# Attention kernel: probabilities turned by DMA in every unit, cache pages copied in three stages, planes and weight parts shared out anew

## What is computed

```python
w = weight[adapter_ids]                                  # 8 of 16 matrices of 512x512
x = x + jnp.einsum('bsi,boi->bso', x, w)                 # layer 0

q = einsum('bsd,ed->bse', x, Wq)                         # 32 heads of 128
k = einsum('bsd,ed->bse', x, Wk); v = ... Wv             # 8 heads of 128
q, k = rope(rmsnorm(q, q_norm_w)), rope(rmsnorm(k, k_norm_w))
kc, vc = k_cache[block_table], v_cache[block_table]      # 16 pages of 32 rows a sequence
scores = q @ concat(kc, k).T * SCALE, cache rows beyond cache_seqlens masked
o = softmax(scores) @ concat(vc, v)                      # 4 query heads share a key head
x = x + einsum('bse,de->bsd', o, Wo)                     # layer 1
```

## Time and profile before

| what | value |
|---|---|
| median of 3 runs | 1097.03 us (1094.78 to 1098.75) |
| profiled execution, its time | 1094.0 us |
| its span, first to last instruction | 1092.0 us |
| granted TensorE clock, mean | 0.97 of full speed |
| busy, us: TensorE, VectorE, GpSimd, ScalarE | 977.4, 920.3, 863.5, 796.4 |
| SyncE's DMA queue, share of 16 engines' span | 65.5% |
| ScalarE's DMA queue | 6.1% |
| moved | 173.69 MB in 505733 packets |

### The profile page before, as it was taken

How to read it: one execution, slowest core, us unless ns; L and a number is a source line. 1 busy time by engine, 2 the same in 40 slices (tenths; PEclk the granted TensorE clock), 3 DMA queues, 4 the chain that set the end, 5 groups by cost and what they waited for, 6 DMA issues and landing times.

```text
span 1092.0 us, 20813 instructions
## 1 busy us (share of the span) xinstructions
PE 977.4 (90%) x5617; PEld 559.3 (51%) x5617; DVE 920.3 (84%) x1942; ACT 796.4 (73%) x2202; POOL 863.5 (79%) x1184
## 2 busy tenths in 40 slices
PE   6787997789868999989998999899998999899997
PEld 4344554455434555545554555455555555455554
DVE  6576876578868999989997999979997999899994
ACT  4364655468677888878887888878887888777873
POOL 3656567558858998889898998889888988989881
PEclk9889999899999999999999999999999999999999
DMA  8688977738897777766778677876776777757862
GB/s 256 174 230 239 246 229 221 207 106 160 179 187 137 142 154 157 138 136 142 158 140 162 128 144 157 148 145 140 154 139 139 153 158 140 130 99 133 152 140 64
DMA packets 505733, 173.69 MB, mean 159 GB/s; under 512 B 429121, under 2 KB 487762, under 8 KB 505618
## 3 DMA queue, kind: packets, MB, share of 16 engines
q1 hardware_dynamic: 482752, 149.76, 65.5%
q10 hardware_dynamic: 21714, 20.25, 6.1%
q0 software_dynamic: 1152, 2.36, 0.8%
HBM read 98.11 MB, written 31.86 MB: 119 GB/s over the span
## 4 chain that ended last, share of the span: by engine, by line
PE 42%; DVE 19%; issue 4%; POOL 2%; ACT 2%; DVEq 0%; POOLq 0%; ACTq 0%
PE S L1729 10%; DVE pr L1359 5%; DVE pr L1331 5%; DVE sm L1344 4%; PE Y L1655 4%; PE Y L1657 4%; PE Y L1656 4%; PE Q L1656 3%; PE Q L1655 3%; PE Q L1657 3%; PE O L1655 2%; PE O L1656 2%; PE O L1657 2%; PE T L1661 2%; POOL wl L644 2%
## 5 line engine op out<-in xcount | busy, mean ns | idle before, releaser
L1359 DVE SCALAR_TENSOR_TENSOR pr<-pr,rc,upper 128x640 f16<-128x640 f32 x220 | 235.2, 1069 | 20.5 <-ACT upper L1025 13.8
L1331 DVE CUSTOM_DVE_ANT_0 pr<-S,mask,rst 128x640 f32<-128x640 f32 x256 | 224.4, 876 | 30.8 <-PE S L1729 19.2
L1025 ACT ACTIVATE upper<-pr,rc 128x640 f16<-128x640 f32 x220 | 170.3, 820 | 75.7 <-DVE rc L1347 75.6
L1045 ACT ACTIVATE pr<-pr,nb 128x640 f32<-128x640 f32 x256 | 209.6, 819 | 17.5 <-DVE nb L1331 14.5
L1729 PE MATMUL S<-kh,qh 128*128 128x320 f16 x512 | 113.0, 303 | 41.9 <-DVE nb L1331 41.9
L754 POOL TENSOR_TENSOR m<-m 128x512 f32<-128x512 f32 x63 | 81.7, 1297 | 78.1 <-DVE m L1403 78.1
L1729 PE MATMUL S<-kl,qh 128*128 128x320 f16 x512 | 112.3, 301 | 0.9 <-POOL kl L644 0.9
L1729 PE MATMUL S<-kh,ql 128*128 128x320 f16 x512 | 112.5, 302 | 0.0
L644 POOL TENSOR_TENSOR wl<-wraw,wh 128x512 f16<-128x512 f32 x71 | 104.2, 1468 | 5.9
L1729 PEld LDWEIGHTS S<-kh,qh 128*128 128x128 f16 x512 | 45.9, 99 | 116.1 <-DVE nb L1331 71.1
L1655 PE MATMUL Q<-wh,xh 128*128 128x512 f16 x256 | 99.9, 390 | 4.1 <-issue 2.8
(11 more groups left out here) (218 smaller groups left out, 2719.4 us busy)
## 6 DMA issues: line engine op xcount, KB each, us to landing
wraw<-in_wall SPq DMA_DIRECT2D x74, 256.0 KB, 3.5
cache_rows<-in_kv ACTq DMA_DIRECT2D x80, 224.0 KB
rawk<-cache_rows SPq DMA_DIRECT2D x55, 256.0 KB
vraw<-cache_rows SPq DMA_DIRECT2D x55, 256.0 KB, 4.6
cache_rows<-in_kv SPq DMA_DIRECT2D x36, 224.0 KB
second<-in_lw SPq DMA_DIRECT2D x4, 1024.0 KB
first<-in_lw SPq DMA_DIRECT2D x3, 1024.0 KB
cache_rows<-in_kv SPq DMA_DIRECT2D x16, 192.0 KB, 3.6
```

The costliest lines, as they stand in the source:

```text
L1025: e.activation(upper16[:, g, :], pr[:, slot(u, g), :], ACT.Copy, scale=rc[:, u % 2, g:g + 1]).then_inc(a_f1, 1)
L1045: e.activation(pr[:, slot(u, g), :], pr[:, slot(u, g), :], ACT.Exp, bias=nb[:, u % 2, g:g + 1], scale=-1.0, accum_out=sm[:, u % 2, g:g + 1 ...
L1331: e.tensor_tensor_reduce(pr[:, slot(u, g), :].rearrange("p (a n) -> p a n", a=2), S[:, :, 0:320], mask[:, u % NB, :].rearrange("p (a n) -> ...
L1359: e.scalar_tensor_tensor(out=lower16(u, g), in0=pr[:, slot(u, g), :], scalar=rc[:, u % 2, g:g + 1], in1=upper16[:, g, :], op0=ALU.mult, op ...
```

## The change

- Every unit's probabilities go through `upper_plane`, `lower_plane` and four DMA transposes, into a new tile `turned`. `norm`, `turn_p` and the per-unit `p_hi` and `p_lo` go; the last unit keeps its own way through TensorE.
- NL is 4: only units 0 to 3 load page by page. The copy is in three stages (rows of heads 0 to 2, of 3 and 4, of 5 to 7), all issued by SyncE: four groups of four pages a period in periods 0 to 7, two groups a period in periods 8 to 39, so 384 DMAs of 4 or 6 rows (64 or 96 KB) where there were 132.
- SyncE's order in a period is new: values, x and mask, the low plane's first pair, keys, weights, half of the copies, the second pair of both planes, the other half, the high plane's first pair.
- Of a head's ten parts, 0, 2, 5, 6 and 8 are made into `wl` by VectorE in one instruction (`split_chunk`), the others by GpSimd in two as before; each is subtracted one period after its rounding, and parts 4 and 5 are rounded in period -3 instead of -2. The squares go to a tile of their own; `wh` and `wl` have 16 places instead of 20.
- The keys' high plane is rounded by ScalarE straight from the raw keys (`keys_hi`), the factors of the scores are made there too (`score_scales`). The values' planes are GpSimd's in all units. Two additions before `norm`'s power become one.
- VectorE's `q_lo` now comes after `new_k_lo`, ScalarE's `new_k_hi` after `upper_plane(i, 1)`, and `scaled_recip(w, 1)` opens the period as before it closed it. Layer 0's products and transposes use T instead of Y, KV and Q.

The diff, cut to its core. Of the last two loops (ScalarE's and VectorE's) only the new side is shown.

```diff
-T_BANK = (0, 1, 0, 0, 1)
-NL = NB + 1
-NA = 8
+NL = 4
...
-COPY_SP = (0, 1, 1, 1, 1, 1, 1, 2, 0, 1, 1, 1, 2, 0)
-COPY_ACT = (2, 2, 3, 2, 2, 3, 3, 2, 1, 0, 0, 0, 0, 0)
-NGRP = NPG // 4
+WRING = 16
...
-HI_ACT = {(0, 6): (1, 0), (0, 7): (1, 0), (0, 8): (1, 1), (0, 9): (1, 1),
-          (1, 0): (-4, 0), (1, 1): (-4, 1), (1, 2): (-3, 0), (1, 3): (-3, 1),
-          (1, 4): (-2, 0), (1, 5): (-2, 1),
-          (1, 6): (0, 0), (1, 7): (0, 1), (1, 8): (1, 0), (1, 9): (1, 1),
-          0: (-6, 0), 1: (-5, 0), 2: (-4, 0), 3: (-3, 0), 4: (-2, 0), 5: (-2, 1),
-          6: (-1, 0), 7: (0, 0), 8: (0, 1), 9: (1, 0)}
-LO_DVE = {(0, 6): (1, 1), (0, 7): (1, 1), (0, 9): (1, 1)}
-LO_POOL = {(0, 8): (1, 1), (1, 0): (-4, 0), (1, 1): (-4, 1), (1, 2): (-3, 0), (1, 3): (-3, 1),
-           (1, 4): (-2, 0), (1, 5): (-2, 1),
-           (1, 6): (0, 0), (1, 7): (0, 1), (1, 8): (1, 0), (1, 9): (1, 1),
-           0: (-6, 1), 1: (-5, 1), 2: (-4, 1), 3: (-3, 1), 4: (-2, 0), 5: (-2, 1),
-           6: (-1, 1), 7: (0, 0), 8: (0, 1), 9: (1, 1)}
-LOAD_AT = {(1, 0): -7, (1, 1): -7, (1, 2): -6, (1, 3): -6, (1, 4): -5, (1, 5): -5,
-           (1, 6): -4, (1, 7): -3, (1, 8): -3, (1, 9): -2,
-           0: -10, 1: -10, 2: -9, 3: -9, 4: -8, 5: -7, 6: -6, 7: -5, 8: -5, 9: -4}
...
+HI_ACT = {(0, 6): 0, (0, 7): 0, (0, 8): 0, (0, 9): 0,
+          (1, 0): -5, (1, 1): -5, (1, 2): -4, (1, 3): -4, (1, 4): -3, (1, 5): -3,
+          0: -6, 1: -5, 2: -5, 3: -4, 4: -3, 5: -3, 6: -1, 7: -1, 8: 0, 9: 0}
+DVE_CHUNKS = (0, 2, 5, 6, 8)
+LO_DVE = {k: at + 1 for k, at in HI_ACT.items() if chunk(k) in DVE_CHUNKS}
+LO_POOL = {k: at + 1 for k, at in HI_ACT.items() if chunk(k) not in DVE_CHUNKS}
+LOAD_AT = {(1, 0): -8, (1, 1): -8, (1, 2): -7, (1, 3): -7, (1, 4): -7, (1, 5): -6,
+           0: -10, 1: -10, 2: -9, 3: -9, 4: -8, 5: -7, 6: -6, 7: -5, 8: -4, 9: -4}
...
+STAGE_ROWS = (slice(0, 6), slice(6, 10), slice(10, 16))
+
+
+def stage_of(hk):
+    return 0 if hk < 3 else 1 if hk < 5 else 2
+
+
+def copies_of(period):
+
+
+    if 0 <= period < 8:
+        return [(0, (period + NL) % NB, t) for t in range(4)]
+    if 8 <= period < 40:
+        n = period - 8
+        return [(1 + n // 16, n % 16 // 2, 2 * (n % 2) + t) for t in range(2)]
+    return []
...
-        pth = sb("pth", [P, 3, G * P], F16)
-        ptl = sb("ptl", [P, 3, G * P], F16)
+        turned = sb("turned", [P, 4, 5 * G * P], F16)
...
-            for i in range(0, NA):
-                if 2 <= i + 1 < NB:
+            for i in range(0, NU + 2):
+                w, early = i - 1, i < NB
+                copied = copies_of(i)
+                if NL <= i + 1 < NU:
+                    load_v(i + 1)
+                if early and i + 3 < NB:
+                    load_x(i + 3)
+                if early and 2 <= i + 1 < NB:
                     load_mask(i + 1)
+                if 0 <= w < LAST:
+                    turn_lower(w, 0)
+                if not early and i + 3 < NU:
+                    load_k(e, i + 3)
                 next_weights(i)
-                if i + 3 < NL:
-                    for t in range(NT):
-                        load_kt(e, kt_regs, i + 3, t)
-
-                        if t == (1 if i else 0) and i + 3 < NB:
-                            load_x(i + 3)
-                else:
-                    load_k(e, i + 3)
-                for b, t in copies_of(i):
-                    copy_pages(b, t)
-
-            for i in range(NA, NU + 2):
-                if NA <= i - 1 < LAST:
-                    turn_upper(i - 1, 1)
-                    turn_lower(i - 1, 1)
+                if i == 0:
+                    for t in range(2, NT):
+                        load_kt(e, kt_regs, 3, t)
                 if i - 3 >= NU - NB:
                     store(i - 3)
-                next_weights(i)
-                if i + 3 < NU:
+                for part in copied[0:len(copied) // 2]:
+                    copy_pages(*part)
+                if 0 <= w < LAST:
+                    turn_upper(w, 1)
+                    turn_lower(w, 1)
+                for part in copied[len(copied) // 2:]:
+                    copy_pages(*part)
+                if early and i + 3 >= NL:
                     load_k(e, i + 3)
-                for b, t in copies_of(i):
-                    copy_pages(b, t)
-                if NL <= i + 1 < NU:
-                    load_v(i + 1)
                 if i < LAST:
                     turn_upper(i, 0)
-                    turn_lower(i, 0)
...
             def keys_scaled(j):
-                e.wait_ge(g_kvs, j + 1)
+                e.wait_ge(made_kh, j + 1)
                 scaled(raw_k(j), raw_k(j), k_scale(j)).then_inc(g_km, 1)
 
-            def keys_hi(j):
-                if j >= 2:
-                    e.wait_ge(p_s, 4 * (j - 1))
-                e.wait_ge(g_km, j + 1)
-                e.tensor_copy(kh[:, j % 2, 0:512], raw_k(j)).then_inc(g_kh, 1)
-
             def keys_lo(j):
-                e.wait_ge(g_kh, j + 1)
-                minus(kl[:, j % 2, 0:512], raw_k(j), kh[:, j % 2, 0:512]).then_inc(g_kc, 1)
+                e.wait_ge(g_km, j)
...
-            def score_scales(j):
-                e.wait_ge(g_pow, j + 1)
-                e.wait_ge(g_kvr, j + 1)
-                e.wait_ge(v_qs, 1)
-                e.wait_ge(g_qr, 2)
-                e.tensor_scalar(rst[:, j % 2, 0:G], pw[:, j % 2, 0:G], f32(kvr[:, j % 2, 1:2]),
-                                f32(qr[:, :]), ALU.mult, ALU.mult).then_inc(g_rst, 1)
...
+            for i in range(0, NU + 1):
                 j, w = i + 1, i - 1
                 nxt = j < NU
+                gathered = 1 <= j < NL
                 w_backs(i - 1)
+                if j < NB:
+                    unit_scales(0, slice(j, j + 1))
+                if gathered:
+                    for t in range(2 if i else 4):
+                        if i or t >= 2:
+                            gather_v(j, t)
                 kv_scales(j)
-                values_scaled(w)
-                values_hi(w)
+                if w >= 0:
+                    values_scaled(w)
+                    output_back(w)
+                    values_hi(w)
+                    values_lo(w)
                 if nxt:
                     keys_scaled(j)
-                output_back(w)
-                values_lo(w)
-                if nxt:
+                if i == 0:
+                    keys_lo(j)
                     q_sum(j)
                     norm(j)
-                    keys_hi(j)
-                    keys_lo(j)
-                    score_scales(j)
-                split_w(i, 0)
-                split_w(i, 1)
-                unit_scales_at(i)
+                    for part in (0, 2, 3):
+                        rope_part(0, part)
+                else:
+                    split_w(i)
+                    if nxt:
+                        q_sum(j)
+                        norm(j)
+                        keys_lo(j)
+                if gathered and i:
+                    for t in range(2, 4):
+                        gather_v(j, t)
+                if i + 2 < NB:
...
+            def keys_hi(j):
+                e.wait_ge(g_kvs, j + 1)
+                if j >= 2:
+                    e.wait_ge(p_s, 4 * (j - 1))
+                e.activation(kh[:, j % 2, 0:512], raw_k(j), ACT.Copy, scale=k_scale(j)
+                             ).then_inc(made_kh, 1)
+
+            def score_scales(j):
+                e.wait_ge(g_pow, j + 1)
+                e.wait_ge(g_kvr, j + 1)
+                if j >= 2:
+                    e.wait_ge(v_max, 4 * (j - 1))
+                e.activation(rst[:, j % 2, 0:G], pw[:, j % 2, 0:G], ACT.Copy,
+                             scale=f32(kvr[:, j % 2, 1:2])).then_inc(a_rst, 1)
 
...
+            for i in range(0, NU + 2):
                 j, w, o, lb = i + 1, i - 1, i - 2, i + 2
+                real, nxt = i < NU, j < NU
+                if 0 < i < NU:
                     v_squares(i)
+                if i > 0 and j < NB:
+                    l0_hi(j)
                 if o == LAST:
                     last_output_hi(0)
                     last_output_hi(1)
+                elif o >= 0 and w != LAST:
                     output_hi(o)
+                if 0 <= w < LAST:
+                    upper_plane(w, 2)
+                if i > 0:
+                    w_squares(i)
+                if i == 0:
+                    exp(i, 0)
+                    l0_hi(j)
+                    v_squares(i)
+                    exp(i, 1)
                 if nxt:
                     k_squares(j)
+                if 0 <= w < LAST:
+                    upper_plane(w, 3)
+                if nxt:
                     new_v(j)
+                if 0 < i and i + 2 < NU:
+                    key_squares(i + 2)
+                if nxt:
+                    keys_hi(j)
+                if 0 < i < NU:
                     exp(i, 0)
                     exp(i, 1)
                 if nxt:
                     q_squares(j)
                 if i < LAST:
                     upper_plane(i, 0)
```

(46 more changed lines are left out.)

750 lines of the change are left out of this document (231 added, 519 removed), and 3 rows, old and new, of the table SQUARES.

## The result

The changed kernel takes 1195.41 us (1193.27 to 1197.49), the kernel before beside it 1096.22: ratio 1.090, 95% interval 1.087 to 1.093. I had predicted 1082, range 1022 to 1120. Its profiled execution spans 1191.5 us (1092.0 before). Times are medians of the executions in the fast state: one of x10's four took 1644.9 us at a mean granted clock of 0.56 and is left out, so that x10 stands at 1105.6 here where the expectations say 1107.7.

The account below looks back on a forecast made before the run. SyncE's queue was to pace units 0 to 39, replacing TensorE's floor: start 32.8, units 0 to 7 186.4, 8 to 39 505.6, 40 to 62 319.7, tail 32.4, outside 2.0, sum 1078.9; plus 3 is 1082 us, range 1022 to 1120.

Parts of the forecast that it names:

- the late units: Units 40 to 63: 13.9 us each, 319.7 us for 23 units, 17.5 less than before.
- (a): At each head's start: 4.4 us waiting for weight part 5's lower plane, made last on GpSimd; expected to go.
- A: The forecast: SyncE's queue paces units 0 to 39, 1082 us; chance 0.42.
- The loop's path: Units 8 to 39: values product, new key, lower plane, SyncE's transposes, loads and copies, next values product; 15.9 us.
- SyncE's list: Units 8 to 39: SyncE's instructions take 14.0 us a unit, 15.4 with a 1.4 us hold behind `rawk`.
- 15.8, near the longer: Units 8 to 39: unit time taken from counts of 15.4 and 15.9; 505.6 us for 32 units.
- Rival C: Units 8 to 39: copies ahead of `turn_upper(w, 1)` delay its landing by queued data; loop 17.0, 1120 us; chance 0.20.
- the early list: Units 0 to 7: SyncE's list takes 23.3 us a unit, 186.4 in all, 7.0 less than before.
- Ends 20.5 and 25 (transposes slowed): Units 0 to 7: range of the unit time, 20.5 us with cheap issues, 25 with transposes slowed.
- (b): Ordinary units: about 0.66 us of TensorE stop before the second score group, VectorE's L1344 held; 0.3 kept.
- Rival B: SyncE hides, units 8 to 39 take 14.2 us; 1031 us, chance 0.25.
- Rival D: GpSimd holds the weight parts on VectorE, +0.4 us a unit in 23 units; 1091 us, chance 0.13.

Follow-up runs that it names:

- x10: Changed kernel with norm ahead of scaled keys, two copy stages instead of three, and half the copies of periods 0 to 7 from ScalarE: 1105.6 us.
- x5: Kernel before, with only weight parts 4 and 5 of the next head made one or two periods earlier: 1074.68 us, ratio 0.980.
- x1: Changed kernel, with all eight copies a period issued behind SyncE's second pair of transposes from period 8 on: 1188.05 us, ratio 1.085.
- x14: x10, with half the copies of periods 8 to 23 issued by ScalarE behind its second upper plane: 1105.79 us, ratio 1.010.
- x15: x14, with SyncE's four remaining copies of periods 8 to 23 moved behind its second pair of transposes: 1082.30 us, ratio 0.989.
- x11: Changed kernel, with every copy of periods 8 to 39 issued in as many pieces but an eighth of the bytes: 1193.03 us, ratio 1.091.
- x2: Changed kernel without any copies from period 8 on, heads 3 to 7 reading rows of heads 1 and 2: 1114.71 us, ratio 1.018.
- x3: Changed kernel, with GpSimd's scaled keys behind norm instead of ahead from period 1 on: 1176.93 us, ratio 1.077.
- x4: Kernel before, with parts 4 and 5 earlier and five weight parts of heads 2 to 7 on VectorE: 1074.77 us, ratio 0.983.
- x9: x4, with the keys' upper plane on ScalarE from unit 9 on and GpSimd's norm ahead of scaled keys: 1063.07 us, ratio 0.970.
- x12: x5, with the keys' upper plane on ScalarE and GpSimd's norm ahead of scaled keys, five parts left on GpSimd: 1064.96 us, ratio 0.972.
- x7: Changed kernel, with heads 3 to 7 copied in one ten-row stage in periods 8 to 23, two stages not three: 1165.29 us, ratio 1.063.

## Why the prediction was wrong, step by step

**Right.** What bounds the late units and the two gains there: the stall at the head's start (a) is gone, as x5 shows by itself (22 us of the 26 expected), and its cause was part 5's place in the order. An issue costs 0.55 us whatever its size (554 ns in the median over 384 copies; the earlier trace rows gave 559 over 52): even the 8 KB ones. The mechanism of the forecast, A, is right too: SyncE's queue is 96% occupied in units 8 to 39 and without a gap in units 0 to 7. The loop's path was the right one, and so was its order; its pieces in the unit shown are 4.3, 1.5, 2.0, 3.6, 1.5 and 3.6, sum 16.5, against 15.9.

**Wrong 1: the terms of SyncE's list in units 8 to 39 were too small (66.7 us).** I had 15.4 for the list; it is 17.2 in the mean of these units. Term by term, measured against forecast: the eight copies 6.0 instead of 5.1, since from the start of one to the start of the next it is 0.75 us, not 0.64 (0.55 is the issue alone; four copies from 701.95 to the transpose at 704.85 are 2.90); the four transposes 6.0 instead of 5.3 (1446 ns in the median for L527, and up to 3.1 us); the two gaps of register loads 1.9 instead of 1.3, since 0.65 (as in the earlier trace rows, 0.67) becomes 1.33 behind a transpose; weights 1.5 instead of 1.0 (1.18 us in the median over 74, instead of 0.76); keys and values 1.2 instead of 0.8. Together these are 3.2 us more than the 14.0 that I had, and the 1.4 that I had added for a hold of the copies behind `rawk` did not cover them. SyncE's issues by line, changed kernel (ns min/median/max):

```profile
L420 SPq DMA_DIRECT2D cache_rows<-in_kv x384: 553/554/1541, 51.7 to 818.6; - x192
...
L527 SPq DMA_TRANSPOSE turned<-upper x126: 1255/1446/3078, 64.9 to 1166.7; - x126
```

The other 0.6 us of the unit are the gaps ahead of L535: I took "15.8, near the longer" of 15.4 and 15.9, but in 21 of 32 units SyncE, full in the mean, still waited for the lower plane. My reading of that is that with two lengths so close whose steps vary from unit to unit, the period is not the longer of the means, since each late step of either is paid; x1, x14 and x15 fit it, and no run shows it by itself. Rival C had the side (slower, 1120), by luck: it takes the copies ahead of `turn_upper(w, 1)` for the cause, and x1 moved them behind for 7 us at most. Its reason, queued data, doesn't hold for the changed kernel's copies by their bytes (x11), but does for the longer ones of x15.

**Wrong 2: the clock was left out.** I counted TensorE's work at full clock. In units 8 to 39 its busy time is 27 us longer than in x2. Not all of that is on the loop: behind 9 of the 32 waits for turned planes the products ran at the lower level, at some 1.3 us more up to `turn_k`, by estimate 9 x 1.3 = 12 us.

**Wrong 3: the early list (24.8 us).** Forecast 23.3 a unit, measured 26.4. In the unit from 121.70 to 150.02 of the changed kernel, one of 28.3 us, the sixteen copies with their gaps took 14.4 us instead of 12.9 (again the 0.75 a copy), and the four transposes 9.0 instead of 5.5. One of them stands behind the loads of x, weights and mask:

```profile
126.39 0.42 SPq L552 DMA_DIRECT2D mask<-mask_rows  x1
126.91 4.06 SPq L536 DMA_TRANSPOSE turned<-pr  x1
```

"Ends 20.5 and 25 (transposes slowed)" named it and didn't reach it.

**Wrong 4: the late units (22.6 us).** Forecast 13.9, measured 14.9. Of (b) I kept 0.3 and named "three engines above 95% passing delays on", without looking for the chain. L1344 (now L1244) is indeed free:

```profile
L1244 DVE TENSOR_SCALAR sm<-sm x126: 151/156/1096, 53.1 to 1164.2; 128x2 f32<-128x2 f32 x126
```

so (b) went and a new wait took its place: norm behind scaled keys behind ScalarE. x3 puts 15 of the 18.5 us of this right (20 units by 0.74), and x3's 14.3 is still 0.4 above my 13.9. There my floor was too low: 13.6 is TensorE's work in units without weights, and in x3's units 40 to 59 TensorE alone is busy 13.9 us a unit. The earlier trace rows had said so, 112.26 us for eight units, 14.0 each.

**Rival B** (1031) had the Trainium skill's rule on issuing for it, and x11 is the answer. **Rival D** fell: with the parts on VectorE or on GpSimd the time is the same within the intervals (x4 and x5, x9 and x12). The Trainium skill's rule for it (SBUF — State Buffer, "Who interferes with whom") is not refuted by that: parts on VectorE took 0.75 us in the median in the changed kernel and 1.75 at most (43 of them), so a part was held now and then, and no time shows it.

**The range** ended at 1120 because I let the two ends of one stretch stand for all: the ends of the early units, of the loop and of the late units were each passed by the measured values at once (25, 17.2 and 13.6 + 0.9 = 14.5 against 26.4, 17.9 and 14.9).

**Still open**: whether it is the bytes or the pieces of the 160 KB copies that slow the transposes in x7 and x15; why a copy's registers take twice as long to load behind a transpose; and what the norm's order alone would bring to the kernel before.

## What to carry over

Before work is moved to a queue because its engine "has time", write down for each instruction what stands behind it on that queue and whether that lies on the loop that has a length of one period: 2.3 us of issues a unit cost 44 us ahead of ScalarE's upper plane and nothing inside a wait of the same engine. Where a list and a loop come out within a microsecond of each other, forecast above both, and expect that mending one of them alone shows nothing. And price small DMAs by their number, from the start of one issue to the start of the next: 64 KB and 8 KB cost the issuing engine the same, and it was 0.75 us, not the 0.55 of the issue. Before you call a queue free, see whether its waits are gaps between its instructions.

## What the runs showed of the hardware that I had not expected

**TensorE's clock can be at its lower level after a wait.** The first values products after a wait of 4.66 us took 0.59 instead of 0.38, and the window over them has a granted clock of 0.50, the lower of its two levels (1.2 GHz); in the other unit shown, after 2.90 us, it was 1.00. Of the 32 such waits in units 8 to 39, 9 (3.0 to 5.6 us long) were followed by products of 0.55 to 0.59 us and 23 (0.7 to 4.3 us) by products of 0.38, so the length of the wait alone doesn't tell.

```profile
480.09 0.59 PE L1502 MATMUL O<-turned,vh 128*128 128x512 f16 x1 [4.66 <-DMA turned<-pr]
```

```profile
693.40:695.80 2.40, 2.31 (x12) 1.16 (x13) 0.28 (x3) 0.65 (x2) 0.02 (x1) 1.00 0.48 131
...
480.00:482.40 2.40, 2.31 (x6) 0.89 (x7) 0.00 (x0) 0.00 (x0) 0.00 (x0) 0.50 0.26 71
```

Where the clock has fallen, a wait on a loop is paid twice, since those products are on the loop themselves: 12 matmuls began in 2.4 us at full clock, 6 at half, and `turn_k` starts 2.59 us behind the first product (482.68) instead of 1.32 (694.81).

**A load of registers behind a transpose costs twice the gap** (1.33 us at 707.78 against 0.65 at 701.30 in the unit above; 1.36 in the median of the 40 that stand behind a transpose in the changed kernel), so the place of a load in the queue is a cost of its own.
